# Second product of a per-channel MLP in token-major order, its result carried back through HBM (one Trainium2 core)

## The chip, the cores and the metric

The kernel runs on one core of one Trainium2 chip. The metric is the device time of one execution in microseconds (us). Before the change the median of 3 runs is 576.02 us (575.11 to 578.19). TensorE (PE) multiplies, VectorE (DVE), ScalarE (ACT) and GpSimd (POOL) work on elements, and SyncE (SP) only issues DMAs; ACT issues some too.

## The reference

Four residual layers on a tensor of 4 images, 8 channels, 256 x 256, in float32. Each layer normalises over groups of two channels (mean and variance over a group of one image) and adds a branch to x:

```python
x = x + conv3x3(_gn(x), L0_weight) + L0_bias
x = x + conv3x3(_gn(x), L1_weight) + L1_bias
h = gelu(einsum('bend,edf->benf', _gn(x), w1) + b1)   # D=256 -> F=1024, exact gelu
x = x + einsum('benf,efd->bend', h, w2) + b2          # one w1, w2 per channel e
x = x + conv3x3(_gn(x), L3_weight) + L3_bias
```

In the third layer a channel is an "expert" with its own weights, and a row of an image (256 values) is a token.

## The kernel before

Layout. x stays in SBUF as X (128 partitions x 4 images x 4096). A partition is (w, c, r): column parity w, channel c, row r within a block of 8 rows; the free axis is (t, j), 32 blocks of rows by 128 column pairs. A chunk is 512 elements (4 values of t), 8 chunks an image. Every f32 operand is split into two f16 parts (high and low), and a product is three f16 matmuls.

Steps. Layers L0 and L1 are conv steps g = 0 to 7, the last layer is steps 8 to 11 (one image each, image g % 4). A conv step: ACT writes the normalised image twice, as the high part into XN and whole into SCR (`normalise_piece`, L439 and L444, five pieces a step), POOL subtracts (L360, the low part), SP copies edge rows into HALO (L242; for a few halves ACT issues the "thirds" of them), PE runs `centre` (L878, three matmuls a chunk) and `tiles` (L885 to L900), and DVE adds the sum to X (`conv_update`, L665). Step 11 shares its buffer with step 8. Before a step's pieces its statistics must be there: DVE bn_stats of every chunk (L626), aggregate (L631), two small group matmuls on PE (`group_mean` L852, `group_variance` L857) with DVE's `deviation` and `variance` behind them, and POOL's `scale_and_bias` (L344 to L351).

The MLP. Images form two pairs. For expert e and pair p, `hidden` (L978) computes hidden-unit-major results: 8 tiles ft of 128 units x 512 tokens, each 6 matmuls; ACT applies gelu (L476) and DVE splits into HID (L732, L735; in the ending ACT writes the high part, L566, and DVE L778). `output` (L1007) has the weight block W2S (128 x 128) stationary and HID (512 tokens) moving, for two halves h of the 256 outputs; ACT copies the result to YT with its bias (L502, L575). Experts 1 to 5 run in a hardware loop: both hidden phases, then both outputs. Experts 6 and 7 run in an order written out (ENDING, L35), four parts: (6, pair 0), (7, pair 0), (6, pair 1), (7, pair 1), so that images 0 and 1 are complete after the second part. The weights W1F and W2F come by SP (L303, L308), and are split by ACT (L472) and DVE (L688).

The way back. A result in YT has output columns on partitions; `result_transposes` (L952, 4 transposes of 128 x 128 f32 a chunk, into one of two PSUM banks) turn it to X's layout, and DVE's `mlp_chunk` adds it to X (L681) and takes its bn_stats (L626). These stand between the matmuls of the third and fourth parts and of steps 8 and 9. Every engine runs its list in order, a wait holds up all behind it. At the end ACT stores images 0 to 2 (L598) and SP image 3 (L325).

## Time and profile before

| | |
|---|---|
| runs | 576.02 us median (575.11 to 578.19) |
| profiled execution | 576.91 us, its span 575.1 us |
| mean granted TensorE clock | 0.971 |
| PE, DVE, ACT, POOL busy | 520.0, 374.1, 291.8, 159.1 us |
| DMA | 57.41 MB, HBM read 30.03 MB, written 8.39 MB |
| stages | 0 to 178 us convs and first expert, to 437 experts, to 499 the last two parts, to 564 last convs, to 575 stores |

PE's matmuls are pipelined, so its busy time says that it had work, not that it ran at its peak. What bounds a stage is read from the waits and from the chain that ended last.

### The profile page before, as it was taken

To read this page: it belongs to the slowest core of one execution; us is meant where nothing else is said; L and a number is where in the kernel's file an instruction comes from. 1 tells how busy PE (TensorE), PEld (TensorE's weight loads), DVE (VectorE), ACT (ScalarE), POOL (GpSimd) and SP (SyncE) were. 2 spreads that over 40 slices of the span, in tenths; PEclk is the share of its full clock that TensorE was granted. 3 is DMA by queue.
4 is the path that set the end of the run, shared out by engine and by line. 5 is a ranking of instruction groups with operands and counts; after the bars stand their busy time and mean duration, and the time that the engine had idled before them with its cause. 6 is when DMAs were issued, how large, how long until landed. Compare 5 with 4: busy or idle time off the path is not lost.

```text
span 575.1 us, 9042 instructions
## 1 busy us (share of the span) xinstructions
PE 520.0 (90%) x3326; PEld 255.5 (44%) x3326; DVE 374.1 (65%) x644; ACT 291.8 (51%) x354; POOL 159.1 (28%) x181
## 2 busy tenths in 40 slices
PE   0879999896979999999999999999999989978990
PEld 0534445364544444444444444444444545445440
DVE  4969999888766395194293392481547598678541
ACT  2599988333635453353362361461444828766510
POOL 4679888853270000000000000000000001677610
PEclk9889999898899999999999999999999999989996
DMA  8845555533020122022011112102123300134769
GB/s 327 324 111 146 150 132 139 143 101 147 0 75 1 73 74 74 0 73 73 0 73 73 31 42 73 73 0 73 74 74 108 112 0 2 45 81 107 242 200 349
DMA packets 14168, 57.41 MB, mean 100 GB/s; under 512 B 3116, under 2 KB 3244, under 8 KB 11052
## 3 DMA queue, kind: packets, MB, share of 16 engines
q1 hardware_dynamic: 11820, 49.30, 26.9%
q10 hardware_dynamic: 2316, 7.68, 3.7%
q8 instruction: 21, 0.34, 0.3%
q14 instruction: 11, 0.09, 0.0%
HBM read 30.03 MB, written 8.39 MB: 67 GB/s over the span
## 4 chain that ended last, share of the span: by engine, by line
PE 62%; DVE 19%; ACT 5%; POOL 4%; DMA 3%; issue 2%; ACTq 1%; SPq 1%; POOLq 0%; DVEq 0%
PE PS L1007 28%; PE PS L978 27%; DVE X L665 6%; DVE ST L626 6%; PE PS L878 2%; POOL XN L360 2%; ACT XN L439 2%; PE PS L952 2%; DMA X<-x 2%; PE PS L936 2%; PE PS L885 1%; DVE X L681 1%; ACT SCR L444 1%; DVE XT L674 1%; DVE SM L641 1%
## 5 line engine op out<-in xcount | busy, mean ns | idle before, releaser
L978 PE MATMUL PS<-XT,W1S 128*128 (+1 forms) x768 | 172.0, 383 | 1.7 <-DVE XT L674 1.7
L1007 PE MATMUL PS<-HID,W2S 128*128 128x512 f16 x768 | 170.8, 379 | 1.6 <-DVE W2S L688 1.6
L476 ACT ACTIVATE SCR<-PS,CONST 128x512 f32<-128x512 f32 x128 | 87.0, 686 | 64.4 <-PE PS L978 27.8
L978 PEld LDWEIGHTS PS<-XT,W1S 128*128 128x128 f16 x768 | 75.6, 99 | 91.1 <-issue 4.7
L1007 PEld LDWEIGHTS PS<-HID,W2S 128*128 128x128 f16 x768 | 75.1, 98 | 87.5 <-issue 1.8
L360 POOL TENSOR_TENSOR XN<-SCR,XN 128x1024 f16<-128x1024 f32 (+1 forms) x61 | 100.4, 1670 | 26.5 <-ACT SCR L444 26.5
L688 DVE SCALAR_TENSOR_TENSOR W2S<-W2F,W2S 128x2048 f16<-128x2048 f32 x10 | 22.9, 2291 | 114.6 <-ACT W2S L472 114.6
L333 POOL MEMSET HALO<- 48x520 f16 x12 | 6.3, 526 | 316.8 <-PE PS L978 316.3
L626 DVE BATCH_NORM_STATS2 ST<-X 128x6 f32<-128x512 f32 x128 | 81.5, 681 | 9.4 <-DMA X<-x 8.2
L439 ACT ACTIVATE XN<-X,SC 128x1024 f16<-128x1024 f32 (+1 forms) x61 | 64.1, 1050 | 33.9 <-POOL SC L351 27.6
L665 DVE SCALAR_TENSOR_TENSOR X<-PS,X 128x512 f32<-128x512 f32 x96 | 59.7, 680 | 21.5 <-PE PS L900 21.5
L878 PE MATMUL PS<-XN,CWT 128*128 128x512 f16 x288 | 72.1, 400 | 1.0 <-POOL XN L360 1.0
L885 PE MATMUL PS<-XN,CWT 64*64 64x512 f16 x288 | 68.3, 385 | 4.1 <-DMA HALO<-XN 3.9
L898 PE MATMUL PS<-HALO,CWT 49*64 49x512 f16 (+1 forms) x288 | 68.7, 385 | 0.0
L900 PE MATMUL PS<-HALO,CWT 49*64 49x512 f16 (+1 forms) x288 | 68.7, 385 | 0.0
L735 DVE SCALAR_TENSOR_TENSOR HID<-SCR,HID 128x512 f16<-128x512 f32 x96 | 66.4, 692 | 3.3
L887 PE MATMUL PS<-XN,CWT 64*64 64x512 f16 x288 | 68.3, 385 | 0.0
L444 ACT ACTIVATE SCR<-X,SC 128x1024 f32<-128x1024 f32 (+1 forms) x61 | 63.9, 1048 | 2.4 <-POOL XN L360 1.9
L502 ACT ACTIVATE YT<-PS,CONST 128x512 f32 (+1 forms) x24 | 16.5, 687 | 88.7 <-PE PS L1007 88.7
L732 DVE TENSOR_SCALAR HID<-SCR 128x512 f16<-128x512 f32 x96 | 40.6, 423 | 8.8 <-ACT SCR L476 5.7
L878 PEld LDWEIGHTS PS<-XN,CWT 128*128 128x128 f16 x288 | 28.3, 104 | 38.2 <-issue 9.7
L885 PEld LDWEIGHTS PS<-XN,CWT 64*64 64x64 f16 x288 | 29.4, 108 | 33.7 <-issue 6.5
(47 smaller groups left out, 442.9 us busy)
## 6 DMA issues: line engine op xcount, KB each, us to landing
W1F<-w SPq DMA_DIRECT2D x10, 1024.0 KB, 4.7
W2F<-w SPq DMA_DIRECT2D x10, 1024.0 KB, 4.8
HALO<-XN SPq DMA_DIRECT2D x48, 129.9 KB
out<-X ACTq DMA_DIRECT2D x12, 512.0 KB, 6.8
HALO<-XN SPq DMA_DIRECT2D x48, 121.8 KB
X<-x SPq DMA_DIRECT2D x2, 2048.0 KB, 19.0
HALO<-XN SPq DMA_DIRECT2D x42, 64.9 KB
HALO<-XN SPq DMA_DIRECT2D x42, 60.9 KB
```

Source lines behind the costliest of these rows:

```text
L360: pool.tensor_tensor(XN[s][:, 1, rows, 1:NJ + 1], SCR[:, m % 2, 0:n * CH].rearrange("p (t j) -> p t j", j=NJ), XN[s][:, 0, rows, 1:NJ + 1] ...
L439: act.activation(XN[s][:, 0, i * TC:(i + n) * TC, 1:NJ + 1], src.rearrange("p (t j) -> p t j", j=NJ), ACT.Identity, bias=SC[:, k, 1:2], sc ...
L444: act.activation(SCR[:, m % 2, 0:n * CH], src, ACT.Identity, bias=SC[:, k, 1:2], scale=SC[:, k, 0:1]).then_inc(xn_ok, 1)
L476: act.activation(SCR[:, ft % 2, 0:CH], bank(ft % G_RING), ACT.Gelu, bias=BT[:, ds(e * FT + ft, 1)], scale=1.0 / (XS * WS)).then_inc(gelu_o ...
L626: dve.bn_stats(ST[:, n % 4, slot], src).then_inc(bn_ok, 1)
L665: dve.scalar_tensor_tensor(out=xc, in0=bank(conv_bank(q)), scalar=1.0 / (XS * WS), in1=xc, op0=ALU.mult, op1=ALU.add).then_inc(x_new, 1)
L878: pe.matmul(to, CWT[:, w, l, 0:P], XN[s][:, part, rows, 1:NJ + 1], start=(n == 0), stop=False)
L885: odd = pe.matmul(bank(k, HALF_P, P), CWT[0:HALF_P, w, l, SIDE:EDGE], XN[s][0:HALF_P, part, rows, 2:NJ + 2], start=False, stop=last)
L898: even = pe.matmul(bank(k, 0, HALF_P), CWT[0:kh, w, l, EDGE:CWN], HALO[s][0:kh, part, rows, 0:NJ], start=False, stop=last)
L900: odd = pe.matmul(bank(k, HALF_P, P), CWT[HALF_P:HALF_P + kh, w, l, EDGE:CWN], HALO[s][HALF_P:HALF_P + kh, part, rows, 0:NJ], start=False, ...
L978: mm = pe.matmul(bank(ft % G_RING), W1S[:, w, h * NF + ft * P:h * NF + (ft + 1) * P], rhs, start=(n == 0), stop=(n == 3 * DH - 1))
L1007: mm = pe.matmul(bank(G2_BANK + h), W2S[:, w, ft * NW + h * P:ft * NW + (h + 1) * P], HID[slot][:, part, ft], start=(ft == 0 and part == 0 ...
```

## The change

The second product turns its operands round: the stationary operand is HID (128 tokens), the moving one is W2S (256 outputs). A pair has four blocks k of 128 tokens, and each is 24 matmuls of 256 columns. ACT copies each block (128 x 256, no bias) to YT or, for expert 7, to SCR or YL; SP stores it to an HBM array yd in X's layout, with runs of 512 B. The transposes are gone: four DMAs an image (two for experts 0 to 6, two for expert 7) bring yd back as YX with X's own partitions, and DVE adds it from SBUF (`add_outputs`). The bias b2 is added to X by DVE in the loop (`add_bias`, experts 1 to 4). XT is laid out anew so that a block's tokens are contiguous. In the last layer 7 PSUM banks go round instead of 5, ACT issues the thirds of step 8 and stores image 1 ahead of step 11's pieces, and DVE does all eight updates of step 8 ahead of image 3's adds.

Three places where instructions move. On PE, third and fourth part of the ending, before (L978 first product, L1007 second product, L952 result transposes; "W2S" and "HID" are their operands):

```order
L1007 MATMUL PS<-HID_59,W2S 128x512 x48
L978 MATMUL PS<-XT,W1S 128x512 x30
L952 MATMUL PS<-CONST,YT 128x128 x4
L978 MATMUL PS<-XT,W1S 128x512 x18
L952 MATMUL PS<-CONST,YT 128x128 x4
L1007 MATMUL PS<-HID_58,W2S 128x512 x6
L952 MATMUL PS<-CONST,YT 128x128 x4
```

And now, from the same place (L1089 first product, L1118 second product, L977 and L982 the group matmuls):

```order
L1118 MATMUL PS<-W2S,HID_60 128x256 x96
L1089 MATMUL PS<-XT,W1S 128x512 x48
L1118 MATMUL PS<-W2S,HID_59 128x256 x96
L1089 MATMUL PS<-XT,W1S 128x512 x12
L977 MATMUL PS<-MV,CONST 128x1
L1089 MATMUL PS<-XT,W1S 128x512 x12
L982 MATMUL PS<-SM,CONST 128x1
```

No transpose is left between the products; a second product has twice the matmuls at half the columns.

On DVE, step 8's updates and image 3, before (L665 update, L681 add, L626 bn_stats):

```order
L649 TENSOR_SCALAR SM<-PS 128x1
L665 SCALAR_TENSOR_TENSOR X<-PS,X 128x512 x2
L681 TENSOR_TENSOR X<-PS,X 128x512
L626 BN_STATS ST<-X 128x6
L681 TENSOR_TENSOR X<-PS,X 128x512
L626 BN_STATS ST<-X 128x6
L665 SCALAR_TENSOR_TENSOR X<-PS,X 128x512 x4
L681 TENSOR_TENSOR X<-PS,X 128x512
```

And now (L768 update, L785 add from SBUF, L729 bn_stats, L734 aggregate):

```order
L752 TENSOR_SCALAR SM<-PS 128x1
L768 SCALAR_TENSOR_TENSOR X<-PS,X 128x512 x4
L785 TENSOR_TENSOR X<-YX,X 128x512 x4
L729 BN_STATS ST<-X 128x6 x4
L785 TENSOR_TENSOR X<-YX,X 128x512 x4
L729 BN_STATS ST<-X 128x6 x4
L734 BN_AGGR MV<-ST 128x2
```

All updates of step 8 now stand ahead of image 3's adds.

On SP, behind the weights of the third part, before (the weights of the fourth part follow at once, then the last layer's "ones" row):

```order
L303 DMA W1F<-w 128x2048
L308 DMA W2F<-w 128x2048
L298 DMA HALO_54<-ones 2x4160
L242 DMA HALO_54<-XN_52 16x2x1948 x2
L242 DMA HALO_54<-XN_52 16x2x2078 x2
```

And now (L342 a block to yd, L218 an image back):

```order
L363 DMA W1F<-w 128x2048
L368 DMA W2F<-w 128x2048
L218 DMA YX<-yd 56x2x2048 x4
L342 DMA yd<-SCR 128x2x128 x4
L218 DMA YX<-yd 8x2x2048 x4
L363 DMA W1F<-w 128x2048
L368 DMA W2F<-w 128x2048
L342 DMA yd<-YT 128x2x128 x4
L218 DMA YX<-yd 56x2x2048 x2
```

The fourth part's weights now stand behind image 0's and 1's whole way through HBM.

The diff, cut to its core:

```diff
...
-G2_BANK, TR_BANK, STAT_BANK = 4, 6, 5
-L3_BANKS = (1, 2, 3, 0, 4)
+G2_BANK, TR_BANK, STAT_BANK, LAST_STAT_BANK = 4, 6, 5, 6
+L3_BANKS = (1, 2, 3, 0, 7, 4, 5)
...
-THIRDS_BY_ACT = ((0, 0), (11, 0), (11, 1),)
+THIRDS_BY_ACT = ((0, 0), (8, 0), (8, 1), (11, 0), (11, 1))
 RSTD_STEPS = 3
 HALO_HALF = 128
...
 ORDER += [("y", b, i) for b in range(3) for i in range(NCH)]
-ORDER += [("c", 8, i) for i in range(QUAD)] + [("y", 3, 0), ("y", 3, 1)]
-ORDER += [("c", 8, i) for i in range(QUAD, NCH)] + [("y", 3, i) for i in range(2, NCH)]
-ORDER += [("c", g, i) for g in range(9, 12) for i in range(NCH)]
+ORDER += [("c", 8, i) for i in range(NCH)] + [("y", 3, i) for i in range(NCH)]
+ORDER += [("c", 9, i) for i in range(NCH)]
+ORDER += [("c", g, i) for g in range(10, 12) for i in range(NCH)]
...
-        k = 0 if n == 13 else STAT_BANK
+        k = STAT_BANK if n < 12 else LAST_STAT_BANK
...
-        tt = (b % 2) * NT + j * TC
-        return XT[:, b // 2, tt:tt + TC, :, :, part, :].rearrange("p t h c r -> p (t h c) r")
+        t = j * TC % TB
+        blocks = XT[:, b, :, :, part].rearrange("p w c (k r t) -> p (w c) k r t", k=NBLK, r=R)
+        return blocks[:, :, j * TC // TB, :, t:t + TC]
...
-        return bank(TR_BANK + m % 2).rearrange("p (k r) -> p k r", r=R)
...
+        return bank(TR_BANK + m % 2).rearrange("p (t k r) -> p k r t", t=TC, r=R)
...
+    def y_tokens(e, p, k):
         if isinstance(e, int):
-            return YT[:, p, :, dh, e, :]
-        return YT[:, p, :, dh, ds(e, 1), :].rearrange("p t e r -> p t (e r)")
+            return YT[:, 2 * p + k // NBLK, k % NBLK, e]
+        return YT[:, 2 * p + k // NBLK, k % NBLK, ds(e, 1)].rearrange("p e d -> p (e d)")
...
+    def y_last(p, k):
+        if p == 0:
+            return SCR[:, k // 2, CH + k % 2 * NW:CH + (k % 2 + 1) * NW]
+        return YL[:, k]
...
+    def y_image(b):
+        return YX[:, (0, 1, 0, 3)[b] * IMG:((0, 1, 0, 3)[b] + 1) * IMG]
...
+    def load_outputs(queue, b, rows):
+        queue.dma_start(y_image(b)[rows].rearrange("p (k f) -> p k f", k=NBLK),
+                        yd[b][:, rows].rearrange("k p f -> p k f")).then_inc(y_in[b], 16)
+    def load_first_experts(queue, b):
+        for w in range(W2):
+            load_outputs(queue, b, slice(w * HALF_P, (w + 1) * HALF_P - R))
+    def load_last_expert(queue, b):
+        for w in range(W2):
+            load_outputs(queue, b, slice((w + 1) * HALF_P - R, (w + 1) * HALF_P))
...
+        def store_tokens(src, b, k, e, signal):
+            dst = yd[b, k].rearrange("(w c r) (t j) -> c (r t) w j", w=W2, c=NC, j=NJ)[e]
+            sp.dma_start(dst, src.rearrange("p (w j) -> p w j", w=W2)).then_inc(signal, 16)
+        def store_outputs(e, p, first):
+            for k in range(BLOCKS):
+                sp.wait_ge(yt_ok, first + k + 1)
+                store_tokens(y_tokens(e, p, k), 2 * p + k // NBLK, k % NBLK, e, y_out[p])
+        def store_last(n, k):
+            p = ENDING[n][1]
+            b = 2 * p + k // NBLK
+            sp.wait_ge(yt_ok, BLOCKS * (NPAIR * LAST + n) + k + 1)
+            store_tokens(y_last(p, k), b, k % NBLK, NE - 1, last_out[b])
...
+        for e in range(1, LAST + 1):
             load_w1(e)
             load_w2(e)
-        for g in range(8, 12):
+            for p in range(NPAIR):
+                store_outputs(e - 1, p, BLOCKS * (NPAIR * (e - 1) + p))
+        load_w1(LAST + 1)
+        load_w2(LAST + 1)
+        store_outputs(LAST, 0, BLOCKS * NPAIR * LAST)
+        load_w1(LAST + 2)
+        load_w2(LAST + 2)
+        sp.wait_ge(y_out[0], 16 * BLOCKS * (NE - 1))
+        sp.wait_ge(g1_mm, FT * (NPAIR * LAST + 2))
+        for b in range(2):
+            load_first_experts(sp, b)
+        for k in range(BLOCKS):
+            store_last(1, k)
+        for b in range(2):
+            sp.wait_ge(last_out[b], 16 * NBLK)
+            load_last_expert(sp, b)
+        load_w1(LAST + 3)
+        load_w2(LAST + 3)
+        store_outputs(LAST, 1, BLOCKS * (NPAIR * LAST + 2))
+        sp.wait_ge(x_new, X_NEW_AT["y", 0, NCH - 1])
+        sp.wait_ge(y_out[1], 16 * BLOCKS * (NE - 1))
+        load_first_experts(sp, 2)
+        load_ones(0)
+        store_last(3, 0)
+        store_last(3, 1)
+        sp.wait_ge(last_out[2], 16 * NBLK)
+        load_last_expert(sp, 2)
+        halo_half(8, 0)
+        store_last(3, 2)
+        store_last(3, 3)
+        halo_half(8, 1)
+        sp.wait_ge(last_out[3], 16 * NBLK)
+        load_last_expert(sp, 3)
...
+        def copy_out(to, k, done):
+            act.wait_ge(g2_mm, done)
+            act.activation(to, bank(G2_BANK + k % 2)[:, 0:NW], ACT.Copy,
+                           scale=1.0 / (HS * WS)).then_inc(yt_ok, 1)
...
+        for n in range(3):
+            ending_hidden(n)
+            for k in range(BLOCKS):
+                ending_out(n, k)
         ending_hidden(3)
...
+        act.wait_ge(y_out[1], 16 * BLOCKS * (NE - 1))
+        act.wait_ge(g1_mm, NE * NPAIR * FT)
+        load_first_experts(act, 3)
+        slot_free(8)
+        normalise_piece(FIRST_PIECE[8])
+        ending_out(3, 0)
+        normalise_piece(FIRST_PIECE[8] + 1)
+        ending_out(3, 1)
+        normalise_piece(FIRST_PIECE[8] + 2)
+        normalise_piece(FIRST_PIECE[8] + 3)
+        ending_out(3, 2)
+        thirds(8, 0)
+        normalise_piece(FIRST_PIECE[8] + 4)
+        ending_out(3, 3)
+        thirds(8, 1)
         for g in range(9, 11):
             normalise(g)
         store(0)
+        store(1)
         slot_free(11)
         for k in range(4):
             normalise_piece(FIRST_PIECE[11] + k)
-        last_thirds(0)
+        thirds(11, 0)
         normalise_piece(FIRST_PIECE[11] + 4)
-        last_thirds(1)
-        for b in range(1, NB - 1):
-            store(b)
+        thirds(11, 1)
+        store(2)
...
-        def mlp_chunk(b, i):
-            m = NCH * b + i
+        def add_outputs(b, i):
+            if i == 0:
+                dve.wait_ge(y_in[b], 16 * 2 * W2)
             xc = x_chunk(b, i)
-            dve.wait_ge(ty_mm, m + 1)
-            dve.tensor_tensor(xc, bank(TR_BANK + m % 2), xc, ALU.add).then_inc(x_new, 1)
+            dve.tensor_tensor(xc, y_chunk(b, i), xc, ALU.add).then_inc(x_new, 1)
+        def mlp_stats(b, i):
             dve.wait_ge(x_new, X_NEW_AT["y", b, i])
-            stats_chunk(12 + b, xc, i)
+            stats_chunk(12 + b, x_chunk(b, i), i)
+        def add_half(b, first):
+            for i in range(first, first + QUAD):
+                add_outputs(b, i)
+            for i in range(first, first + QUAD):
+                mlp_stats(b, i)
+        def add_bias(e):
+            for i in range(NCH):
+                xc = X[:, ds(e * IMG - (IMG - i * CH), CH)].rearrange("p (t j) -> p t j", j=NJ)
+                dve.tensor_tensor(xc, xc, B2.unsqueeze(1).broadcast_to([P, TC, NJ]), ALU.add
+                                  ).then_inc(bias_ok, 1)
...
             next_w1(e + 1)
+            add_bias(e)
...
+            if ft >= 4:
+                add_outputs(0, ft - 4)
         def in_fourth(ft):
+            if ft == 0:
+                deviation(12)
...
             if ft == 2:
-                mlp_chunk(1, 2)
                 variance(12)
-            if ft in (4, 6):
-                mlp_chunk(1, ft // 2 + 1)
...
+            if ft >= 2:
+                add_outputs(1, ft - 2)
...
         w2_parts(LAST + 2)
         ending_hidden(2, in_third)
-        for i in range(2, NCH):
-            mlp_chunk(0, i)
+        next_w1(LAST + 3)
+        for i in range(QUAD):
+            mlp_stats(0, i)
+        add_half(0, QUAD)
         aggregate(12)
-        mlp_chunk(1, 0)
-        mlp_chunk(1, 1)
-        deviation(12)
         w2_parts(LAST + 3)
         ending_hidden(3, in_fourth)
-        for i in range(5, NCH):
-            mlp_chunk(1, i)
+        for i in range(6, NCH):
+            add_outputs(1, i)
+        for i in range(NCH):
+            mlp_stats(1, i)
         aggregate(13)
         deviation(13)
+        add_outputs(2, 0)
+        add_outputs(2, 1)
         variance(13)
-        for i in range(NCH):
-            mlp_chunk(2, i)
+        add_outputs(2, 2)
+        add_outputs(2, 3)
+        for i in range(QUAD):
+            mlp_stats(2, i)
+        add_half(2, QUAD)
         aggregate(14)
         def last_updates(g, i, n):
             for k in range(QUAD):
                 conv_update(g, i + k)
-                if n is not None and k == 0:
+                if n is not None and k == 1:
                     deviation(n)
-                if n is not None and k == 1:
+                if n is not None and k == 3:
                     variance(n)
         last_updates(8, 0, 14)
-        mlp_chunk(3, 0)
-        mlp_chunk(3, 1)
         last_updates(8, QUAD, None)
-        for i in range(2, NCH):
-            mlp_chunk(3, i)
+        add_half(3, 0)
+        add_half(3, QUAD)
         aggregate(15)
...
+            tail = q - 8 * NCH
+            if tail >= len(L3_BANKS):
+                f = q - len(L3_BANKS)
+                pe.wait_ge(x_new, X_NEW_AT["c", f // NCH, f % NCH])
+            elif tail >= 0:
                 pe.wait_ge(gelu_ok, NE * NPAIR * FT)
-                if i == 3:
-                    pe.wait_ge(var_ok, 2 * 14)
-                if i == 4:
-                    pe.wait_ge(yt_ok, 4 * NE)
+                if tail >= 5:
+                    pe.wait_ge(yt_ok, NE * NPAIR * BLOCKS)
             elif q >= RING:
                 pe.wait_ge(x_new, X_NEW_AT["c", (q - RING) // NCH, (q - RING) % NCH])
             to, rows = bank(conv_bank(q)), slice(i * TC, (i + 1) * TC)
...
-        def output(e, p, h, between=None, part_of_end=None):
-            k = p * DH + h
+        def output(e, p, k, between=None, part_of_end=None):
...
+            tokens = slice(k * P, (k + 1) * P)
+            to = bank(G2_BANK + k % 2)
...
-                for part, w in ((0, 0), (1, 0), (0, 1)):
-                    mm = pe.matmul(bank(G2_BANK + h),
-                                   W2S[:, w, ft * NW + h * P:ft * NW + (h + 1) * P],
-                                   HID[slot][:, part, ft],
-                                   start=(ft == 0 and part == 0 and w == 0),
+                for part, w in PRODUCTS:
+                    mm = pe.matmul(to[:, 0:NW], HID[slot][:, part, ft, tokens],
+                                   W2S[:, w, ft * NW:(ft + 1) * NW],
+                                   start=(ft == 0 and part == w),
                                    stop=(ft == FT - 1 and w == 1))
+                if ft == FT - 1:
+                    mm.then_inc(g2_mm, 1)
...
+        for n, (e, p, _) in enumerate(ENDING):
+            hidden(e, p, in_fourth_hidden if n == 3 else None, n)
+            for k in range(BLOCKS):
+                output(e, p, k, in_fourth_output if n == 3 else None, n)
+        for g in range(8, 12):
             before_step(g)
             for i in range(0, NCH, QUAD):
-                last_centres(g, i, None)
+                for k in range(QUAD):
+                    if g < 10 and i + k == NCH - 1:
+                        group_mean(g + 6)
+                    centre(g, i + k)
+                    if (g, i, k) == (8, 0, 0):
+                        group_variance(13)
+                if g < 10 and i > 0:
+                    group_variance(g + 6)
                 tiles(g, i)
...
```

## Rows read from the trace of the kernel before

**Rows 1.** The page's section 4, the chain that ended last: shares of the span by engine

```profile
PE 62%; DVE 19%; ACT 5%; POOL 4%; DMA 3%; issue 2%; ACTq 1%; SPq 1%; POOLq 0%; DVEq 0%
```

**Rows 2.** Busy time by window: us, then busy and (count) per engine, clock, DMA share, GB/s

```profile
178.00:437.00 259.00, 259.00 (x1201) 117.40 (x1200) 138.55 (x217) 110.69 (x142) 0.00 (x0) 1.00 0.16 57
437.00:499.00 62.00, 59.90 (x313) 31.37 (x310) 46.25 (x70) 39.18 (x51) 8.53 (x11) 1.00 0.10 35
499.00:564.00 65.00, 54.92 (x552) 28.32 (x552) 43.50 (x76) 32.59 (x33) 34.79 (x35) 0.97 0.58 169
564.00:575.00 11.00, 0.00 (x0) 0.00 (x0) 0.03 (x1) 0.00 (x0) 0.00 (x0) 0.57 0.87 339
```

**Rows 3.** The chain of waits in order of time: start, us, what; second product, halo transfers

```profile
44.61 2.42 DMA HALO<-XN
...
385.26 20.72 PE PS L1007 x96
...
554.84 4.40 DMA HALO<-XN
```

**Rows 4.** Groups by line and shape: busy us, mean ns | idle before

```profile
L1007 PEld LDWEIGHTS PS<-HID,W2S 128*128 128x128 f16 x768 | 75.1, 98 | 87.5 <-issue 1.8
...
L952 PE MATMUL PS<-CONST,YT 128*128 128x128 f32 x128 | 18.7, 276 | 6.3 <-DVE X L681 5.4 <-ACT YT L575 0.9
...
L952 PEld LDWEIGHTS PS<-CONST,YT 128*128 128x128 f32 x128 | 14.9, 141 | 12.8 <-DVE X L681 7.3 <-issue 2.2
...
L681 DVE TENSOR_TENSOR X<-PS,X 128x512 f32<-128x512 f32 x32 | 21.8, 681 | 7.3 <-PE PS L952 7.3
...
L575 ACT ACTIVATE YT<-PS,CONST 128x512 f32<-128x512 f32 x8 | 5.5, 684 | 24.3 <-PE PS L1007 24.3
```

**Rows 5.** Timeline of PE, third, fourth part, step 8: start, us, what

```profile
447.25 6.64 PE L978 MATMUL PS<-XT,W1S 128*128 128x512 f16 x30
...
474.44 0.60 PE L952 MATMUL PS<-CONST,YT 128*128 128x128 f32 x4
474.88 1.46 PE L978 MATMUL PS<-XT,W1S 128*128 128x512 f16 x6
...
497.54 1.46 PE L1007 MATMUL PS<-HID,W2S 128*128 128x512 f16 x6
...
518.15 1.04 PE L952 MATMUL PS<-CONST,YT 128*128 128x128 f32 x8
```

**Rows 6.** Timeline of DVE, third part

```profile
456.82 0.69 DVE L778 SCALAR_TENSOR_TENSOR HID<-SCR,HID 128x512 f16<-128x512 f32 x1 [0.55 <-ACT HID L566]
...
460.86 0.69 DVE L778 SCALAR_TENSOR_TENSOR HID<-SCR,HID 128x512 f16<-128x512 f32 x1 [0.82 <-ACT HID L566]
...
462.79 2.27 DVE L688 SCALAR_TENSOR_TENSOR W1S<-W1F,W1S 128x2048 f16<-128x2048 f32 x1
```

**Rows 7.** Timeline of ACT: pieces of steps 9 and 11; its DMA issues (ACTq)

```profile
507.44 1.24 ACT L439 ACTIVATE XN<-X,SC 128x1024 f16<-128x1024 f32 x1 [5.46 <-POOL SC L351]
...
537.33 1.25 ACT L439 ACTIVATE XN<-X,SC 128x1024 f16<-128x1024 f32 x1 [4.63 <-POOL SC L351]
...
552.72 2.89 ACTq L242 DMA_DIRECT2D HALO<-XN  x4
555.65 9.59 ACTq L598 DMA_DIRECT2D out<-X  x8
```

**Rows 8.** Timeline of DVE: last updates of the kernel

```profile
561.55 2.48 DVE L665 SCALAR_TENSOR_TENSOR X<-PS,X 128x512 f32<-128x512 f32 x4 [3.19 <-PE PS L900]
```

**Rows 9.** DMA issues: count, KB each, median us to landing

```profile
W1F<-w SPq DMA_DIRECT2D x10, 1024.0 KB, 4.7
...
out<-X SPq DMA_DIRECT2D x8, 256.0 KB, 7.7
```

**Rows 10.** PE after a wait for image 2's statistics, and a window behind it

```profile
513.31 0.38 PE L852 MATMUL PS<-MV,CONST 128*128 128x1 f32 x2 [2.80 <-DVE MV L631]
...
515.00:516.00 1.00, 1.00 (x4) 0.34 (x3) 1.00 (x4) 1.00 (x2) 1.00 (x2) 0.50 0.00 0
```

302 lines of the change are left out of this document (115 added, 187 removed).

## The prediction, before the change was run

> **What bounds the kernel now.** I read the chain that ended last first: 62% of the span is PE and 19% DVE [rows 1]. The windows say where. From 178 to 437 us PE is busy all the time at the full clock (2.4 GHz), and no other engine comes near [rows 2]. The chain gives the second product of one expert there as 96 matmuls in 20.72 us [rows 3], 215.8 ns for 512 columns, back to back. From 437 to 499 PE still looks full (59.9 of 62 us), but the timeline shows what with: between the products stand result transposes, and the third and fourth part run from 447.25 to 499.0 [rows 5], 51.8 us for 192 matmuls that take 41.4 at 215.8. From 499 to 564 PE is at work in 54.9 of 65 us and waits on others in turn: the pieces of steps 9 and 11 wait for POOL's scale, so for DVE's statistics, 5.46 and 4.63 us [rows 7], and one group matmul waits 2.80 us for DVE's aggregate, after which PE runs at half its clock (1.2 GHz, 0.50) [rows 10]. The last 11 us hold only DMA, at 339 GB/s and a share of 0.87 [rows 2]: ACT begins to store images 1 and 2 only at 555.65, behind its last halo copies [rows 7], and the last update ends at 564.0 [rows 8]. So four stages with four limits.
>
> **Part by part.** The sum is made against the span of 575.1 us; the profiled execution took 1.8 us more (576.91), and is 0.9 above the median of the runs.
>
> 1. *Second product in 256 columns.* 768 matmuls of 512 become 1536 of 256, with 768 more weight loads. The 215.8 ns are 213.3 of columns at 2.4 GHz and 2.5 fixed, so 256 columns should take 109.2 ns if the load stays hidden: 1536 x 109.2 = 167.7 us in place of 165.7, **+2.0 us**. The trace has no 256-column matmul. Below, half of 215.8 per matmul gives +0. Above, a load that isn't hidden at all adds its 98 ns [rows 4] to each: +153. The nearest row is the result transposes: eight in 1.04 us and four in 0.60 [rows 5], so 110 ns from one to the next, each with a load of 128x128 f32 whose record is 141 ns, longer than the 98 of f16 [rows 4]. A pair of load and matmul thus fits in 110 ns with a heavier load. I take +2.0. If 141 ns were the step, it would be +51.
>
> The Trainium skill, "TensorE: Matmul & The Clock Gate", section "Back-to-back issue gap", says that in a stream of weight load and matmul both set the spacing, with 81 ns at 128 columns against 56 for a matmul alone. If these 25 ns came on top here too, the term would be 1536 x 134 - 165.7 = +40 us, an estimate from that page. The same passage has 131 ns at 512 columns, where this trace shows 215.8, so I don't follow it; the load can also hide behind 107 ns of columns where it can't behind 53.
>
> 2. *Third and fourth part of the ending.* 64 of the 128 transposes stood here, 7 us at 110 ns; 51.8 - 41.4 - 7.0 leaves 3.4 us of waits, part of the 6.3 that the transposes waited in all, mostly for DVE's adds [rows 4]. What is late next? ACT and DVE. In the third part DVE's last low part of HID began at 460.86 [rows 6], while PE, with no transposes, would be through the first block by 460.3: it ends that block at 461.7, 1.2 us late. DVE now has an add behind each of ft = 4 to 7, but their place was free (0.55 and 0.82 us of wait a time, rows 6), so I leave it. Then W1's low part (2.27), four bn_stats, four adds, four bn_stats and the aggregate: `group_mean(12)` on PE, after ft = 1 of the fourth part, stands some 0.6 us, `group_variance(12)` 1 us, and the tail of HID 0.3. Sum: 41.4 + 1.2 + 1.6 + 0.3 = 44.5, **-7.3 us**, with all of point 1 counted by itself. Bounds: -10.4 (no wait at all) and -3 (DVE as slow as it was).
>
> 3. *The loop.* ACT copies four blocks of 256 in place of two of 512 (684 ns, rows 4; half of it is 342, and twice the fixed part makes it dearer, at most 684): at most 2.7 us more an expert, on an engine busy 111 of 259 us [rows 2]. DVE's eight bias adds an expert, at the 681 ns of an add [rows 4], are 5.4 us four times; DVE is busy 139 of 259. Both lie in the phase of the second product, where they wait for PE. SP's stores are 1 MB an expert beside 2 MB of weights; W1 of the next expert is now queued behind the wait for the last block, and lands 4.7 us later [rows 9], with 20.7 to spare. I take 0; if that cover were gone, 4 x 5.4 us.
>
> 4. *The way through HBM.* It is new, and a wait in DVE's queue. The first product of part two ends at 438.7 (with its share of point 1). SP then reads 3.67 MB for images 0 and 1: 10.8 us at 339 GB/s [rows 2], so 449.5; at the 223 GB/s of a lone W1F (1.05 MB in 4.7 us, rows 9) 16.5, so 455.2. The last block of part two is copied at 449.7, its store and the read back take 2.4 us each like a halo copy [rows 3] and 1.2 of issue: image 0 is there by 455.8 or 461.2. DVE wants it behind ft = 4, at 459.1 on this clock. W1 for part four goes out behind that, and lands at 458.5 to 464, wanted at 462.5. I take 0, with 3 us in the range; it would hold up HID's parts 5 to 7, and PE behind them.
>
> 5. *The tail.* PE is through the MLP at 494 instead of 499. Step 8: ACT does pieces, copies, and four halo issues each half (0.7 us each, rows 7), so step 9's pieces start near 506, not at 507.44; ACT is the limit here, and 5 us become 1.4. DVE: image 2 is back at 497.5 (second block of part four copied at 491.8, store, 1.2, read), its adds and statistics end at 508. PE waits for them with `group_mean(14)`, about 3 us, goes down to half the clock as in rows 10, and ends step 8's second half near 515. Then DVE does four updates, eight adds, eight bn_stats of image 3 (10.6 us at 0.6 to 0.7 each) and the aggregate, to 526, and `variance(15)` at 529.5. Step 11's pieces could start at 531, but ACT first stores image 1, which needs step 9's last update (534): it starts at 535, not 537.33, **-2.3**. From there to the last halo copy all is as before, 22 us, except that its transfer took 4.40 us against 2.42 at rest [rows 3]; with image 1 gone by then I take half of this, -1. Last update ends at 560.6, not 564.0.
>
> 6. *The end.* From 555.65 on 6.3 MB were written, 18.6 us at 339 GB/s, which gives 574. Now 4.2 MB are left at about 554: 12.4 us, so 566.5. The last chunk's own way, 560.5 + 1.2 + 4.9 to 7.7 [rows 9], says the same. From last update to end 6.0 us against 11.1: **-5.1**.
>
> Sum: -2.3 - 1.1 - 5.1 = -8.5 us. The 5.3 won by points 1 and 2 are not added: they come to the end only through ACT's and DVE's lists, which keep 2.3 of them. Span 566.6, profiled about 568.3, and on the median's scale **568 us**.
>
> **The rivals.**
> *The load isn't hidden (7%).* For it: 768 more loads, no such matmul in the trace. Against it: 110 ns with a heavier load. At 141 ns 568 + 49 = 617. It turns the sign from 115 ns a matmul on (8 us over 1536).
> *The reads of yd are slow (9%), the case on the other side.* Place: DVE's `add_outputs(0, 0)`, with HID's parts and PE behind it. If 56 partitions a DMA get half of 339 GB/s, the 3.67 MB end at 460.3, image 0 is there at 466.3, 7.2 us late; and image 3's read beside the stores of the last expert makes image 2 3.5 us late on DVE's chain. 568 + 10.7 = 579. It decides from about 220 GB/s down. For it: no row of 56 partitions; against: 8 KB runs like those of W1F.
> *The tail takes all (10%).* DVE's chain from image 2 to the statistics of image 3 grows by another clock fall at step 9 (its half of `tiles` at 1.2 GHz, 2.6 us more) and image 1's store delays step 11's pieces to 538. Then only the end's store backlog is won: 573 to 575.
> *More is won (14%).* The halo copies of step 8 and image 2 arrive as computed but PE keeps its clock, and ACT's chain moves with PE's 5 us: 561 to 563.
> *The forecast (60%):* 568, its own range 564 to 573.
>
> **How the numbers follow.** A change under 0.5% (2.9 us) can't be told from none here. Faster (below 573.1): 60 + 14 and half of the third rival, 5, is 79%. Same: the other half and the edge of the second, 7%. Slower: 7 + 7 = 14%. The range 561 to 579 holds the forecast, the third and fourth, and the slow reads; it leaves the unhidden load and a little at each end.
>
> **What would show it.** Right: the 96 matmuls of an expert's pair of second products, now 192, at 20.9 to 21.0 us in the loop; PE's third and fourth part in 45 to 47 us; no wait of DVE's add for a DMA in the third part; step 11's first piece near 535; last update near 560; 4 MB written in the last 12 us. Wrong: a second product over 22 us an expert (point 1), `add_outputs` waiting on a DMA before 462 (point 4), a last update before 557 or after 564 (point 5), or more than 9 us from the last update to the end (point 6).

## The result: 595.4 us, slower by 3%, and the profile after

The changed kernel takes 595.38 us (592.06 to 597.35, 4 runs), the kernel before 577.11 beside it (575.11 to 578.24, 4 runs): a ratio of 1.0315, with a 95% interval of 1.0255 to 1.0374. The forecast was 568, the range 561 to 579, and the time lies outside it. The profiled execution took 596.14 us with a span of 594.3; its mean granted clock is 0.949, before 0.971. In what follows "part one to four" are the four pieces of the MLP's ending, and line numbers of the profile after are those of the changed kernel or of the experiment named.

The chain that ended last, to be read beside [rows 1]:

```profile
PE 52%; DVE 25%; DMA 9%; ACT 5%; POOL 4%; issue 3%; ACTq 2%; SPq 1%; POOLq 0%; DVEq 0%
```

The windows, with the columns of [rows 2]:

```profile
178.00:437.00 259.00, 258.44 (x1768) 172.58 (x1767) 156.23 (x245) 111.83 (x164) 0.00 (x0) 1.00 0.25 81
437.00:499.00 62.00, 50.98 (x324) 32.45 (x322) 37.44 (x58) 32.41 (x48) 2.35 (x5) 0.89 0.69 155
499.00:564.00 65.00, 44.82 (x390) 23.38 (x390) 44.58 (x80) 33.90 (x37) 38.24 (x37) 0.82 0.65 173
...
443.00:461.00 18.00, 18.00 (x120) 11.53 (x118) 7.42 (x7) 10.54 (x18) 0.00 (x0) 1.00 0.89 192
463.00:475.00 12.00, 3.46 (x15) 1.89 (x16) 4.30 (x7) 1.32 (x2) 0.00 (x0) 0.58 0.88 160
```

The loop is as it was: PE busy 258.4 of 259 us at the full clock. From 437 on PE has lost 9 us of busy time to waits in 62, and from 499 another 10 in 65. The granted clock of the last row is 0.82 instead of 0.97; no run here separates what that costs from the waits it comes with. The two last lines hold the reason for the first loss: from 443 to 461 the DMA engines are busy (0.89) and move only 192 GB/s, where [rows 2] have 339 at 0.87; from 463 to 475 they are busy still and PE is not.

Four views of that stretch: the timelines of DVE, of PE and of SP's queue, and the DMA issues (count, KB each, median us to landing).

```profile
459.58 0.69 DVE L902 SCALAR_TENSOR_TENSOR HID<-SCR,HID 128x512 f16<-128x512 f32 x1 [0.55 <-ACT HID L671]
469.42 0.69 DVE L785 TENSOR_TENSOR X<-YX,X 128x512 f32<-128x512 f32 x1 [9.15 <-DMA YX<-yd]
```

```profile
470.77 0.82 PE L1118 MATMUL PS<-W2S,HID 128*128 128x256 f16 x3 [8.30 <-DVE HID L902]
```

```profile
439.39 1.78 SPq L218 DMA_DIRECT2D YX<-yd  x4
443.06 8.22 SPq L342 DMA_DIRECT2D yd<-SCR  x4
462.67 1.31 SPq L218 DMA_DIRECT2D YX<-yd  x4
```

```profile
YX<-yd SPq DMA_DIRECT2D x4, 896.0 KB
...
yd<-SCR SPq DMA_DIRECT2D x4, 128.0 KB, 15.1
YX<-yd SPq DMA_DIRECT2D x4, 128.0 KB
```

Read from below: the reads of images 0 and 1 (four of 896 KB, 56 rows each) go out at 439.4 and fill SP's ring (its queue of issued DMAs) until about 460. The last expert's four stores stand behind them, 15.1 us each. SP waits for these stores until 462.67, then reads the last expert's 8 rows a half, and image 0 is whole at 469.42. DVE's first add waits for this, with HID's sixth low part (of eight) behind it in its queue; PE stands 8.30 us for that low part. The third part takes 450.32 to 483.97, 33.7 us.

The tail has the same wait for image 2, and more (timelines of DVE, of GpSimd, here POOL, and of PE):

```profile
517.98 1.29 DVE L785 TENSOR_TENSOR X<-YX,X 128x512 f32<-128x512 f32 x2 [7.50 <-DMA YX<-yd]
...
542.44 6.58 DVE L785 TENSOR_TENSOR X<-YX,X 128x512 f32<-128x512 f32 x4
...
586.81 2.53 DVE L768 SCALAR_TENSOR_TENSOR X<-PS,X 128x512 f32<-128x512 f32 x4 [6.44 <-PE PS L1027]
```

```profile
543.14 7.80 POOL L455 TENSOR_TENSOR XN<-SCR,XN 128x1024 f16<-128x1024 f32 x4 [0.19 <-ACT SCR L541]
```

```profile
520.13 0.63 PE L1012 MATMUL PS<-XN,CWT 64*64 64x512 f16 x1 [7.23 <-DMA HALO<-XN]
...
551.87 0.59 PE L977 MATMUL PS<-MV,CONST 128*128 128x1 f32 x2 [7.87 <-DVE MV L734]
```

The four adds at 542.44 take 6.58 us where four took 2.48 a moment before, and they waited for nothing that the profile shows; GpSimd computes four low parts at the same time. PE's wait of 7.87 us for the aggregate ends right behind these adds and their statistics. The last update ends at 589.3 (before 564.0, [rows 8]) and the span 5.0 us later, before 11.1.

### The profile page after: what moved, and what is told of

Its sections match the earlier page's. It is cut to its first block, busy times and chain, and to the rows that moved or that the text cites. A ratio compares the mean times of both kernels' runs of the same rounds, so it can differ in the third digit from the quotient of the medians.

```text
span 594.3 us, 10531 instructions
## 1 busy us (share of the span) xinstructions
PE 516.0 (87%) x3966; PEld 318.3 (54%) x3966; DVE 393.8 (66%) x676; ACT 294.5 (50%) x386; POOL 164.0 (28%) x181
## 4 chain that ended last, share of the span: by engine, by line
PE 52%; DVE 25%; DMA 9%; ACT 5%; POOL 4%; issue 3%; ACTq 2%; SPq 1%; POOLq 0%; DVEq 0%
PE PS L1118 24%; PE PS L1089 21%; DVE ST L729 7%; DVE X L768 7%; PE PS L1012 3%; DVE X L785 3%; DMA yd<-SCR 2%; DMA W1F<-w 2%; DVE HID L902 2%; ACT XN L536 2%; DMA X<-x 2%; POOL XN L455 1%; PE PS L1063 1%; ACTq L283 1%; PE PS L1005 1%
## 5 line engine op out<-in xcount | busy, mean ns | idle before, releaser
L1118 PE MATMUL PS<-W2S,HID 128*128 128x256 f16 x1536 | 175.4, 276 | 13.6 <-DVE HID L902 10.1
L1089 PE MATMUL PS<-XT,W1S 128*128 (+1 forms) x768 | 170.3, 381 | 1.5 <-DVE XT L777 1.5
L1118 PEld LDWEIGHTS PS<-W2S,HID 128*128 128x128 f16 x1536 | 151.0, 99 | 36.9 <-DVE HID L902 12.4
L1089 PEld LDWEIGHTS PS<-XT,W1S 128*128 128x128 f16 x768 | 75.2, 99 | 88.8 <-issue 3.0
L455 POOL TENSOR_TENSOR XN<-SCR,XN 128x1024 f16<-128x1024 f32 (+1 forms) x61 | 102.8, 1713 | 32.7 <-ACT SCR L541 32.5
L1012 PE MATMUL PS<-XN,CWT 64*64 64x512 f16 x288 | 75.3, 414 | 17.0 <-DMA HALO<-XN 17.0
L432 POOL MEMSET XN<- 128x128 f16 x6 | 2.7, 457 | 313.7 <-PE PS L1118 313.5
L729 DVE BATCH_NORM_STATS2 ST<-X 128x6 f32<-128x512 f32 x128 | 78.8, 675 | 8.3 <-DMA X<-x 8.2
L768 DVE SCALAR_TENSOR_TENSOR X<-PS,X 128x512 f32<-128x512 f32 x96 | 59.7, 679 | 33.2 <-PE PS L1027 33.2
L1025 PE MATMUL PS<-HALO,CWT 49*64 49x512 f16 (+1 forms) x288 | 75.7, 414 | 0.0
L1027 PE MATMUL PS<-HALO,CWT 49*64 49x512 f16 (+1 forms) x288 | 75.7, 414 | 0.0
L1014 PE MATMUL PS<-XN,CWT 64*64 64x512 f16 x288 | 75.3, 414 | 0.0
L602 ACT ACTIVATE YT<-PS 128x256 f32 (+1 forms) x56 | 21.4, 383 | 99.6 <-PE PS L1118 98.9
L1012 PEld LDWEIGHTS PS<-XN,CWT 64*64 64x64 f16 x288 | 31.5, 116 | 51.5 <-DMA HALO<-XN 20.3
```

The costliest lines, as they stand in the source:

```text
L455: pool.tensor_tensor(XN[s][:, 1, rows, 1:NJ + 1], SCR[:, m % 2, 0:n * CH].rearrange("p (t j) -> p t j", j=NJ), XN[s][:, 0, rows, 1:NJ + 1] ...
L729: dve.bn_stats(ST[:, n % 4, slot], src).then_inc(bn_ok, 1)
L768: dve.scalar_tensor_tensor(out=xc, in0=bank(conv_bank(q)), scalar=1.0 / (XS * WS), in1=xc, op0=ALU.mult, op1=ALU.add).then_inc(x_new, 1)
L1012: odd = pe.matmul(bank(k, HALF_P, P), CWT[0:HALF_P, w, l, SIDE:EDGE], XN[s][0:HALF_P, part, rows, 2:NJ + 2], start=False, stop=last)
L1014: even = pe.matmul(bank(k, 0, HALF_P), CWT[HALF_P:P, w, l, SIDE:EDGE], XN[s][HALF_P:P, part, rows, 0:NJ], start=False, stop=last)
L1025: even = pe.matmul(bank(k, 0, HALF_P), CWT[0:kh, w, l, EDGE:CWN], HALO[s][0:kh, part, rows, 0:NJ], start=False, stop=last)
```

## The experiments

Three questions: why are the reads slow; what would the kernel take if they cost nothing; and, since that turned out to be 578 and not 568, what else. The experiments came in five batches, each beside the kernel before, whose median was between 575.6 and 576.8 (577.1 beside the changed kernel); where two kernels of different batches are compared, up to 1.5 us of their difference can come from that. The loop begins up to 3 us earlier or later from execution to execution, so stages are compared by their lengths.

**The reads by themselves.** Behind the changed kernel's last store, groups of reads, each waited for:

```diff
+        for b in (0, 1):
+            probe_load(b, slice(0, 56))
+            probe_load(b, slice(64, 120))
+        landed()
...
+        for b in (0, 1):
+            probe_load(b, slice(0, P))
+        landed()
```

> The changed kernel with ten timed groups of reads of the stored outputs appended behind its last store, each group waited for before the next: (a) two images in rows 0 to 55 and 64 to 119, 3.67 MB in four DMAs, as the kernel reads them; (b) two images in rows 0 to 111, 3.67 MB in two DMAs; (c) two whole images, 4.19 MB in two; (d) 8 rows of one image, 128 KB; (e) 8 rows, 64 KB in runs of 8 KB; (f) the same 64 KB in runs of 512 bytes; (g) the 8 last rows of each half of two images, 512 KB in four DMAs; (h) three images in rows 36 to 91, 2.75 MB; (i) two images by even and by odd rows, 4.19 MB in four; (j) as (a), one half of the rows issued by SyncE, the other by ScalarE. Theory P (the rows a DMA covers set its rate: 56 rows in one half of the partitions reach half of the ways into SBUF): (a) 19 us or about 195 GB/s, (b) 11 to 12 us, (c) 12 to 14, (h) 8 to 10 (rows on both sides of the middle), (i) 12 to 14, (j) 11 to 12; 8 rows are slow, (d) 3.5 to 5 us and (g) 6 to 7. Theory H (reading back what was stored, in runs of 8 KB, is limited in HBM or by the descriptors): (a), (b), (c), (h), (i) and (j) all run at 190 to 200 GB/s, so (b) 19, (c) 21, (h) 14. Theory Q (the reads were slow because the kernel's own work stood beside them): (a) at 300 GB/s or more here, 12 us.

The first issue of each group, so that a group's time is the distance to the next line (with the wait for landing), and below it three windows, inside (a), (c) and (h):

```profile
590.66 1.73 SPq L427 DMA_DIRECT2D YX<-yd  x4
...
612.32 0.81 SPq L427 DMA_DIRECT2D YX<-yd  x2
...
627.36 0.90 SPq L427 DMA_DIRECT2D YX<-yd  x2
...
639.86 0.29 SPq L427 DMA_DIRECT2D YX<-yd  x1
...
648.76 1.30 SPq L427 DMA_DIRECT2D YX<-yd  x4
...
658.69 1.19 SPq L427 DMA_DIRECT2D YX<-yd  x3
```

```profile
592.00:612.00 20.00, 0.00 (x0) 0.00 (x0) 0.00 (x0) 0.00 (x0) 0.00 (x0) 0.50 0.83 178
628.00:638.00 10.00, 0.00 (x0) 0.00 (x0) 0.00 (x0) 0.00 (x0) 0.00 (x0) 0.50 0.98 381
...
660.00:668.00 8.00, 0.00 (x0) 0.00 (x0) 0.00 (x0) 0.00 (x0) 0.00 (x0) 0.50 0.83 327
```

(a) as in the kernel 21.7 us, (b) rows 0 to 111 15.0, (c) all rows 12.5 for more bytes, (g) four times 8 rows 9.9, (h) 56 rows across the middle, three images, 10.2. (d) took 3.8, (e) and (f) 2.5 and 2.6, (i) 13.4, (j) 16.3. The same number of rows moves 178 GB/s in one half and 327 across the middle, at the same busy share of 0.83. That excludes Q (nothing ran beside them) and H. P is right in kind, but its figures for (b), 11 to 12 us, for (g), 6 to 7, and for (j), 11 to 12, were too low: a second ring takes a quarter off (a), not half.

> The changed kernel with eight timed groups of reads behind its last store, each waited for: (a) rows 0 to 119 of two stored images, 3.93 MB in two DMAs; (b) rows 8 to 127, the same size; (c) rows 0 to 63 of two, 2.1 MB; (d) rows 32 to 95 of two, 2.1 MB; (e) two whole images of the input x, 4.19 MB; (f) x in rows 0 to 55 and 64 to 119, 3.67 MB in four DMAs; (g) x in rows 36 to 91 of two, 1.84 MB; (h) one image of x in sixteen DMAs of 8 rows, 2.1 MB. So far: two whole stored images 12.5 us, rows 0 to 111 15.0, rows 0 to 55 and 64 to 119 21.7, three times rows 36 to 91 10.2, 8 rows 3.8. Theory P (what counts is which partitions the rows of a DMA are, and nothing in HBM): (f) takes as long as with the stored outputs, 21 to 22 us, (e) 12 to 13; (c) rows in one half are slow, 11 to 13 us, (d) the same size across the middle 7.5 to 8.5; (g) 7 to 8; (h) about 2 us for each DMA, 30 to 35; (a) and (b) 13 to 14. Theory E (what counts is how many rows, and so how the 16 engines are filled): (c) and (d) the same, 8 us, (a) and (b) slow like in the kernel, 20 us. Theory H (HBM): everything read from x is fast, (f) 12 us.

```profile
595.46 0.84 SPq L427 DMA_DIRECT2D YX<-yd  x2
617.21 0.81 SPq L427 DMA_DIRECT2D YX<-yd  x2
638.92 1.32 SPq L427 DMA_DIRECT2D YX<-yd  x2
651.36 1.25 SPq L427 DMA_DIRECT2D YX<-yd  x2
...
672.07 1.90 SPq L432 DMA_DIRECT2D YX<-x  x4
693.50 0.75 SPq L432 DMA_DIRECT2D YX<-x  x2
```

From x, which nobody stored, 56 rows a half take 21.4 us again (f), so it isn't HBM. Rows 0 to 63 take 12.4 us (c), rows 32 to 95 with the same bytes 8.1 (d), (e) 12.6, (g) 7.0, (h) 2.1 us for each DMA of 8 rows. So P holds for these. But (a) and (b), 120 rows, took 21.7 us each, as E had it and P not: it isn't the half alone. The Trainium skill, "SBUF — State Buffer", section "Door 1: The DMA port swizzle", says that partitions 0 to 63 reach 8 of SBUF's 16 DMA ports and 8 neighbours two; (c), (d) and (h) agree with it. The Trainium skill, "DMA: Bandwidth & Descriptors", section "The descriptor swizzle", says that in a transfer of 128 partitions each engine writes a port of its own. With that, 120 rows would lose this dealing. No run here shows which engine wrote where, so for the 120 rows it is an account that was not shown. Nor is it whole: 112 rows aren't 128 either, and they took 15.0 us, between the two.

**The reads in the kernel.**

```diff
-        for w in range(W2):
-            load_outputs(queue, b, slice(w * HALF_P, (w + 1) * HALF_P - R))
+        load_outputs(queue, b, slice(0, P - R))
...
+            sp.wait_ge(y_in[b], 16)
```

> Each image is read back in one DMA of rows 0 to 119 instead of two of 56 rows (the last expert's rows 56 to 63 come along with old data and are read again later, as before; its four stores wait until that read has landed; expert 0's outputs are also stored into the last expert's rows early in the loop, eight more stores). Theory P (56 rows in one half read at half rate): the 3.9 MB for images 0 and 1 land about 453 instead of 459.5, the last expert's rows of image 0 by 462 instead of 469.4, VectorE's wait for them falls from 9.2 us to about 2, and the kernel takes 584 to 589 us. Theory H (a limit in HBM): the reads land at 460 or later, and the time is 595 to 600 us. Theory T (the tail's new order is what costs, not the read): 593 to 596, whatever the reads do.

594.84 us (594.17 to 596.00), ratio to before 1.0316 (1.0287 to 1.0345): no gain, DVE's wait 9.96 us. P missed; the time lies in T's range and just under H's, and at the time this spoke for H. The bare reads of 120 rows, measured after it, show why.

```diff
-            load_first_experts(sp, b)
+            load_outputs(sp, b, slice(0, HALF_P - R))
...
+                if k == 1:
+                    act.wait_ge(y_out[0], 16 * BLOCKS * (NE - 1))
+                    for b in range(2):
+                        load_outputs(act, b, slice(HALF_P, P - R))
```

> The lower half of images 0 and 1 (rows 64 to 119) is issued by ScalarE's queue while SyncE's reads rows 0 to 55; nothing else changes. Theory P: the two halves use different ways into SBUF and run beside each other, all four land by 453 instead of 459.5, the four stores queued behind them on SyncE's ring land by about 454, image 0 is whole at 462 to 464, and the kernel takes 585 to 590 us. Theory H: the rate stays at 195 GB/s over both rings, 594 to 597 us. Theory T: 593 to 596.

590.42 us (588.23 to 592.42), ratio 1.0230 (1.0198 to 1.0263): 5 us better, just over the slow end of what P expected (585 to 590). SP's last reads go out at 459.1 instead of 462.7. The third edit, here against the first of the three:

```diff
-        load_outputs(queue, b, slice(0, P - R))
+        load_outputs(queue, b, slice(0, P))
```

> Each image is read back in one DMA of all 128 rows (the last expert's rows with old data, and again in two DMAs of 8 rows, as before; expert 0's outputs are stored into the last expert's rows once, early in the loop; the last stores wait for the landing of that read). Rows 0 to 119 gained nothing in the kernel (594.84), while two whole images took 12.5 us by themselves. Theory P: 4.2 MB for images 0 and 1 land about 452 to 453 instead of 459.5, image 0 is whole at 461 to 463 instead of 469.4; 586 to 589 us. Theory Q (beside the kernel's own work no read is faster than 195 GB/s): the reads land at 461, 595 to 598 us.

586.14 us (584.84 to 587.32), ratio 1.0187 (1.0165 to 1.0208), as P expected. Eight more rows than in the first of these, and 8.7 us less. Its SP queue, its first add, and the window with the reads:

```profile
437.10 0.89 SPq L218 DMA_DIRECT2D YX<-yd  x2
445.07 5.97 SPq L341 DMA_DIRECT2D yd<-SCR  x4
451.09 2.03 SPq L218 DMA_DIRECT2D YX<-yd  x4
```

```profile
457.91 0.69 DVE L787 TENSOR_TENSOR X<-YX,X 128x512 f32<-128x512 f32 x1
```

```profile
437.00:450.00 13.00, 12.47 (x107) 10.04 (x105) 4.99 (x6) 5.71 (x8) 0.00 (x0) 1.00 0.90 341
```

The add waits for nothing now; DVE's only wait for a read is 4.6 us, for image 2.

**No read at all.** This bounds what the way through HBM costs.

```diff
     def load_outputs(queue, b, rows):
+        return
...
-            dve.tensor_tensor(xc, y_chunk(b, i), xc, ALU.add).then_inc(x_new, 1)
+            dve.tensor_tensor(xc, xc, xc, ALU.add).then_inc(x_new, 1)
```

> No output is read back: the eight reads of each kind are left out, VectorE adds X to itself in place of the outputs (so the outputs' values are left out of the result; the instructions and their operands' sizes stay), and does not wait for a read; the stores and the waits for them stay. It bounds what the way through HBM costs. Theory P and H alike: VectorE's wait of 9.2 us, TensorE's of 8.3, the 7.5 us before image 2's adds and 7.2 before step 8's second half go, and the kernel takes 565 to 572 us. Theory T (the tail's order, the busier VectorE and the half clock cost most): still over 585 us.

577.75 us (576.08 to 579.16), ratio 1.0020 (1.0003 to 1.0036). So reading back, with the waits for it, costs 17.6 us (17.3 if each kernel is held against the kernel before of its own batch); the stores to HBM are still in this kernel. 9.8 are left between it and the forecast. No theory had that; T, over 585, is out. The trace: parts three and four take 448.40 to 494.8, 46.4 us; from there the tail is no shorter than before. PE waited 10.7 us for step 10's halo copies, while images 0 and 1 went out:

```profile
546.69 0.63 PE L1011 MATMUL PS<-XN,CWT 64*64 64x512 f16 x1 [10.71 <-DMA HALO<-XN]
```

Hence:

```diff
         store(0)
-        store(1)
         slot_free(11)
...
+        store(1)
         store(2)
```

> The kernel without the reads back (577.75 us) with image 1's stores put back behind step 11's pieces, as in the kernel before. Theory S (in that run image 1's 2.1 MB of stores filled the DMA engines ahead of step 10's halo copies, and ScalarE spent 10 us on issuing them; TensorE waited 10.7 us): the wait falls to about 1 us and the kernel takes 566 to 570 us, close to the 568 forecast. Theory T2 (the tail is bound by VectorE's order, image 3's adds behind all of step 8's updates): 575 to 578.

576.33 us (574.60 to 577.87), 1.4 less; S expected 8 to 12. PE's wait is still 5.5 us, and the last update now stands 8.1 us before the end (567.8 of 575.9), and 4.5 with the stores early (569.2 of 573.7): the place moves most of the backlog from the middle to the end.

> The changed kernel with image 1's stores alone put back behind step 11's pieces. Theory S: step 11's pieces start at about 556.5 instead of 560.8 and step 10's halo copies meet fewer stores; 588 to 591 us. Theory that the placement costs only where the reads are absent: 594 to 596.

595.68 us (594.92 to 596.57): nothing gained. S falls as the cause, in both kernels.

**GpSimd's scale.** In the tail it stands behind all low parts of the step before; in the loop of steps 2 to 7 behind the third.

```diff
-        low_parts(8)
+        low_parts(8, 0, 3)
+        scale_and_bias(13)
+        low_parts(8, 3)
...
-        scale_and_bias(13)
-        low_parts(9)
+        low_parts(9, 0, 3)
+        scale_and_bias(14)
+        low_parts(9, 3)
```

> Reads back in all 128 rows (586.14 us by themselves), image 1's stores behind step 11's pieces (alone 595.68, no gain), and image 0's adds two slices later in the third part. In the 128-row kernel ScalarE stood 12.4 us for image 1's last update before step 11's pieces, though its scale was there 4.5 us earlier. Theory S2 (the stores' place costs once the reads are out of the way): 580 to 583 us. Theory that the tail's chain of GpSimd takes up what is freed (without the reads it was 577.75 with and 576.33 without that place): 584 to 587.

> As the run before it, and GpSimd computes the scale of steps 9, 10 and 11 behind the third low part of the step before instead of behind its last (where the loop's steps have it). Theory G (the tail is one chain: low parts of a step, then the next step's scale on GpSimd, then ScalarE's pieces, 15 to 19 us a step, so that nothing done earlier on the other engines shows): step 9's pieces start 3 to 4 us earlier and each later step 2 to 4 us more; 570 to 577 us. Theory V (VectorE's adds and updates bound the tail): within 2 us of the run before it.

> Without the reads back (the outputs' values are left out of the result, VectorE adds X to itself), image 1's stores late (576.33 us), and GpSimd's scale of the next step behind the third low part. Theory G: 565 to 570 us, the forecast's own number for a way through HBM that costs nothing. Theory V: 574 to 577.

> As the run before it, with step 8's third copies of the halo issued by SyncE again instead of ScalarE. ScalarE spent 2.7 us on each of the two groups of issues, the first ahead of step 8's last piece. If that delay is part of the chain: 1 to 3 us less than the run before it. If SyncE's queue is then late with them: the same or up to 3 us more.

585.56 us (583.24 to 587.12) without the early scale. That is within the spread of the kernel with 128 rows alone (586.14), so S2 falls too. With the early scale 587.08 (585.98 to 589.91); without reads 575.13 (573.08 to 576.14), and 574.20 (571.82 to 577.64) with step 8's thirds on SP. G expected 570 to 577 beside the reads and 565 to 570 without them. Beside the reads the early scale waits itself: image 1's variance comes behind image 2's first adds on VectorE, and these behind a DMA: GpSimd stood 10.6 us for it. Without reads, where nothing of this kind stands in the way, the early scale is worth 1.2 us, and G's 565 to 570 falls; beside the reads no run had both the early scale and the variance moved ahead. ScalarE's issues are worth 0.9 us by the medians, which ten runs of each don't tell from nothing.

**VectorE's order.** The change's own point: all of step 8's updates ahead of image 3's adds.

```diff
+        variance(13)
         add_outputs(2, 0)
         add_outputs(2, 1)
-        variance(13)
...
+        add_half(3, 0)
         last_updates(8, QUAD, None)
-        add_half(3, 0)
```

> Without the reads back, image 1's stores late (576.33 us: the outputs' values are left out of the result), and VectorE's order as before the change: image 1's variance ahead of image 2's adds, image 3's first four adds between step 8's two groups of updates. Theory V (VectorE's order holds the tail): image 3's statistics are ready 4 to 5 us earlier, 569 to 573 us. Theory D (the halo copies of step 10, behind the stores of image 0, hold it: TensorE stood there and VectorE waited 10 us in that run): 575 to 577.

> Reads of 128 rows, image 1's stores late, image 0's adds later (585.56 us), and on VectorE image 1's variance ahead of image 2's adds. There step 9's scale was ready at 512.3, 19 us after step 8's; before the change it was 17. VectorE stood 4.4 us for image 2's read with the variance behind it. If that is on the chain: step 9's pieces 2 to 4 us earlier, 582 to 584 us. If GpSimd's low parts end later anyway (theirs ended 509.1): no change, 585 to 586.

> As the run before it, and image 3's first four adds and statistics between step 8's two groups of updates, as before the change. TensorE waited 8 us for image 3's statistics at 542.9 in the kernel without it. Theory V: the wait falls to 2 to 4 us, 578 to 582 us. Theory C (the adds and GpSimd's low parts only stretch each other elsewhere): 583 to 586.

The order undone: 579.00 us (577.47 to 580.70) without reads, 2.7 more than with the changed order (576.33, another batch); beside the fast reads 585.28 (584.74 to 588.00) with the variance ahead alone, 586.17 (584.58 to 587.45) with both. V falls: beside the reads the new order costs nothing, and where they are out of the way it is the better one. The trace of e13_order shows what the order runs into instead. VectorE, then GpSimd at the same time:

```profile
530.09 8.07 DVE L788 TENSOR_TENSOR X<-YX,X 128x512 f32<-128x512 f32 x4
```

```profile
532.28 7.80 POOL L458 TENSOR_TENSOR XN<-SCR,XN 128x1024 f16<-128x1024 f32 x4 [0.19 <-ACT SCR L544]
```

Four adds and four low parts, 2.5 and 6.3 us by themselves (4.23 + 2.06 in the next trace), take 8.1 and 7.8. Before the change the adds read a bank of PSUM and X. So:

```diff
+            if b >= 2:
+                xc = xc[:, 0:CH - 2]
+                dve.tensor_tensor(xc, bank(6)[:, 2:CH], xc, ALU.add).then_inc(x_new, 1)
+                return
```

> As the run before it, but the adds of images 2 and 3 take 510 columns of a bank of PSUM in place of the outputs read back (their outputs are left out of the result; the wait for the reads stays), so that VectorE reads SBUF once. Theory C: GpSimd's four low parts of a step take 6.4 us again wherever adds stand beside them (7.5 to 7.8 now), four adds 2.5 us (up to 7.8 now), and the time falls by 2 to 5 us against the run before it. Theory V alone: the same within 1 us.

580.03 us (578.59 to 581.45), ratio to before 1.0054 (1.0030 to 1.0077): 6.1 less than the run before it, more than C's 2 to 5. The same adds and the low parts beside them:

```profile
527.62 2.46 DVE L790 TENSOR_TENSOR X<-PS,X 128x510 f32<-128x510 f32 x4
```

```profile
532.50 4.23 POOL L458 TENSOR_TENSOR XN<-SCR,XN 128x1024 f16<-128x1024 f32 x3 [0.19 <-ACT SCR L544]
537.75 2.06 POOL L458 TENSOR_TENSOR XN<-SCR,XN 128x1024 f16<-128x1024 f32 x1 [1.02 <-ACT SCR L544]
```

Here the low parts stand 1.0 us for ScalarE in their middle, so from the first to the last they take 7.3 us against 7.8: GpSimd is hardly later in the collision. VectorE is: its four adds are 5.6 us longer.

> The changed kernel with three timed groups behind its last store: eight adds of 128x510 on VectorE from SBUF alone; then eight of the same beside four of GpSimd's low parts (128x1024); then eight adds that read PSUM and SBUF beside four low parts. Theory C (two SBUF operands on VectorE and GpSimd's operands share a way in, one at a time): the first 5 us, the second group takes the sum, about 13 us (5 of VectorE, 8.5 of GpSimd), with adds of up to 2.5 us, the third 5 us for VectorE and 8.5 for GpSimd beside it. Theory that the stretched adds in the kernel wait for something else (the DMA writes beside them): the second group is as fast as the first and as the third.

The three groups: alone; eight adds from SBUF beside the last four of GpSimd's eight; eight adds from PSUM beside four.

```profile
594.40 4.89 DVE L995 TENSOR_TENSOR X<-X 128x510 f32<-128x510 f32 x8 [7.73 <-DMA YX<-x]
599.44 18.11 POOL L526 TENSOR_TENSOR XN<-SCR,XN 128x1024 f16<-128x1024 f32 x8 [24.04 <-DVE X L995]
607.57 12.33 DVE L995 TENSOR_TENSOR X<-X 128x510 f32<-128x510 f32 x8 [8.27 <-POOL XN L526]
620.00 4.86 DVE L995 TENSOR_TENSOR X<-PS,X 128x510 f32<-128x510 f32 x8
620.04 8.12 POOL L526 TENSOR_TENSOR XN<-SCR,XN 128x1024 f16<-128x1024 f32 x4 [2.48 <-DVE X L995]
```

4.89 + 8.12 = 13.0 us, and together they took 12.3: nearly the sum, so they ran one at a time but for 0.7 us. From PSUM both ran at their own pace. C is shown. The Trainium skill, "SBUF — State Buffer", section "SBUF: two separate sides", says so: VectorE with two SBUF inputs and a GpSimd operation that reads SBUF lock each other out for a whole instruction.

> Without the reads back, VectorE's order as before the change (579.0 us), and the adds of images 2 and 3 from a bank of PSUM (510 columns; the outputs' values are left out of the result). Theory C: the two groups of four adds that took 7.1 us take 2.5 again, TensorE's waits of 6.1 and 4.1 us go, 569 to 573 us, within 1 per cent of the forecast of 568 for a way through HBM at no cost. Theory D (halo copies hold step 10 anyway): 576 to 579.

575.00 us (573.50 to 576.55), 4.0 less than with SBUF adds (579.0), or 3.5 with each against its own batch; C expected 6 to 10. The stretched adds and TensorE's two waits are gone, as it said, but a part comes back in another place, seen in the timeline of VectorE and in the windows:

```profile
544.86 2.57 DVE L770 SCALAR_TENSOR_TENSOR X<-PS,X 128x512 f32<-128x512 f32 x4 [10.54 <-PE PS L1031]
```

```profile
532.00:536.00 4.00, 3.11 (x20) 1.09 (x12) 2.32 (x4) 1.01 (x1) 2.67 (x5) 1.00 1.00 336
536.00:540.00 4.00, 0.00 (x0) 0.00 (x0) 0.00 (x0) 4.00 (x5) 2.36 (x2) 0.97 0.67 227
540.00:544.00 4.00, 3.32 (x32) 1.49 (x36) 0.00 (x0) 2.56 (x4) 3.92 (x3) 0.50 0.63 162
```

TensorE ends step 9 early, stands idle from 536 to 540 for step 10's halo copies and goes on at 0.50 of its clock (1.2 GHz). The chain that ended last shows what these copies stand behind (three of its pieces), and SP's timeline before the change when they began there:

```profile
529.28 0.60 SPq L285
...
530.87 2.50 SPq L285
...
538.21 2.43 DMA HALO<-XN
```

```profile
530.79 0.61 SPq L242 DMA_DIRECT2D HALO<-XN  x1
```

From 499 to 529 this chain runs over ScalarE and GpSimd, step after step (scale, pieces, low parts). Then SP issues the seven copies one behind the other from 529.28 to 538.16, some in 0.6 us and some in up to 2.50, while image 0's stores go out (DMA share 1.00 from 532 to 536), and the last copy travels 2.43. Before the change the copies began at 530.79, only 1.5 us later, and PE was still at step 9 meanwhile. So D was right for this part: what PE and VectorE gain earlier doesn't reach step 10.

## Why the prediction was wrong, point by point

1. *Second product in 256 columns: right.* An expert's two second products of a pair are 192 matmuls in 20.96 us, 109.2 ns each, as the forecast had them; before 96 in 20.72 [rows 3]. The load's record is 99 ns and stays hidden, so +2.0 us stands and +40 or +51 doesn't.

2. *Third and fourth part, -7.3 us: nearly right.* Without reads they took 46.4 us; 44.5 and 0.5 as their share of point 1 were forecast. 1.9 of it is one wait of PE for ACT's copy of a block, which the sum doesn't have. Nor does it have that parts one and two take 21.6 us each instead of 20.7, because PE is through the first block of 128 tokens before HID's last low part (waits of 0.56 and 0.52).

3. *The loop, 0: right.* Windows as before.

4. *The way through HBM, 0: this is the step that failed.* It priced the reads at 339 or 223 GB/s, from rows of other shapes; they ran at 192. It put the last expert's store and read back at 2.4 us each "like a halo copy"; the stores took 15.1 in the ring behind the reads, the 8-row reads 6.7. So image 0 was there at 469.4, not at 455.8 to 461.2, and what stood behind the add in DVE's queue, HID and with it PE, stood too. The term of 0 measured 17.6 us by the kernel without reads (image 2's wait of 7.5 us in the tail is in this figure). The rival "the reads of yd are slow" named mechanism and place, and even the rate ("half of 339"), but had 579 us and a chance of 9%: its price left out that the stores queue behind slow reads and that 8 rows are slower still. 9.2 of the 17.6 come back with 128 rows, 5.0 with a second ring.

5. *The tail, -3.4: its sign was wrong.* Even without reads the last update ended at 569.2, or 567.8 with image 1's stores late; 560.6 were forecast and 564.0 was the time before. The sum took an add at 0.6 to 0.7 us. From SBUF, beside GpSimd's low parts, four adds take 6.6 to 8.1 us, and VectorE's statistics and PE's group matmul stand behind them. Taking the SBUF operand away was worth 6.1 us beside fast reads and 4.0 without reads, both in VectorE's order of before the change. In the changed kernel as it stands it wasn't run; its trace has one such group, 4.1 us longer than the group before it. The replaced adds read PSUM, and that was the hidden half of what the transposes paid for. The second thing that the sum lacks is a term for step 10's halo copies: it goes from step 9's pieces to step 11's and from there to the last update. Without reads and collisions step 11's first piece did start at 534.99 (535 forecast), but the last update ended at 564.6, because PE stood for step 10's copies until 540.7 and had steps 10 and 11 still to do. The change's order on VectorE, which the forecast weighed, is worth 2.7 us in favour of the change without reads; the late place of image 1's stores 1.4 us without reads and nothing beside them.

6. *The end, -5.1: right in size.* 5.0 us from the last update to the end; 6.0 were forecast, before 11.1. But it was no gain: with image 1's stores back in their old place the last update ended at 585.3, 4.0 earlier, the end came 9.2 us behind it, and the time was the same (595.68). What the end wins, the middle loses.

The sum of what was measured, on the forecast's 568: 17.6 for the reads and 4.0 for the collision give 589.6 of the 595.4. These two are not clean of each other: the kernel without reads still has stretched adds (3.7 and 4.0 us for four), but 575.0, the time with neither, lies only 2.8 below its 577.75. 575.0 is 7.0 over the forecast; in the profiled execution it is 5.8 of span, 4.0 ahead of the last update and 1.8 behind it. Point 2 could give 2.9 of them (1.5 in parts one and two, 1.4 in parts three and four) if they reached the end, which no run tests, ScalarE's issues of step 8's thirds less than 1. The trace of that kernel has PE's wait for step 10's copies there, at the end of a chain over ScalarE, GpSimd and SP. No run took this chain away: neither the early scale without the collision nor image 0's stores behind step 10's copies was tried. So the last 7 us are read from a trace, and their cause stays open.

No version that computes the whole result beat the kernel before. The nearest was e12_variance, 585.28 us. Without reads and outputs the fastest, e10_no_read_thirds, took 574.20, 0.3% less than the kernel before.

## What to carry to other kernels

When an operand moves from PSUM to SBUF, look at who else reads SBUF then: here VectorE's adds took up to three times as long beside GpSimd's, and what stood behind them was late. Of the shapes tried here, all 128 partitions read back fastest, with rows too many rather than in pieces that skip some (12.5 us against 21.7); price a read from a row of the same partitions. The store and the read of the last piece queue behind what is in the ring already (15.1 us here for 128 KB). A wait for a DMA belongs behind the work in the same queue that others need.

## What the runs showed that was not expected

120 of 128 rows in one DMA took 21.7 us for two images and all 128 took 12.5. A DMA of 8 neighbouring rows takes 2.1 us for 128 KB in a row of sixteen, 33.6 us for one image, where two images in all rows took 12.5. And the 128 transposes by TensorE with adds from PSUM, 110 ns each or 14 us in all, were cheaper than they looked: in this form the add and GpSimd's low parts don't hold each other up.
